# One attention step of TensorE in another order, in a fused AdaLN, attention and FFN kernel in three-pass float32

## The reference, cut to what matters

```python
x = x + attn(einsum('bct,bcd->bdt', x, W[style_id]))   # q,k,v projections, clip at 8, layer norm of q and k,
                                                       # 32 heads of 16, ALiBi, causal softmax, output projection
x = x + ffn(einsum('bsi,boi->bso', x, W2[adapter_id])) # up, relu squared, down, routed low-rank part, layer norm
```

## Time and profile before

| | |
|---|---|
| time, median of 3 runs | 1191.57 us (1190.74 to 1194.24) |
| the profiled execution | 1193.86 us, its span 1192.1 us |
| mean granted TensorE clock | 0.988 |
| attention loop in the span | from about 20 us to 627 us, steps 6 to 31 from 107 us on |
| busy: PE, PEld, DVE, ACT, POOL | 96%, 76%, 54%, 46%, 59% |

### The profile page before, as it was taken

One profiled execution on the slowest core, in us unless ns is written; L12 is line 12 of the kernel. 1 busy time (PEld: TensorE's weight loads), 2 busy tenths in 40 slices (PEclk: granted clock), 3 DMA queues, 4 the chain that ended last, 5 costly groups with the idle time before them and its releaser, 6 DMA issues.

```text
span 1192.1 us, 27390 instructions
## 1 busy us (share of the span) xinstructions
PE 1140.6 (96%) x11124; PEld 904.8 (76%) x11124; DVE 644.7 (54%) x1047; ACT 551.9 (46%) x910; POOL 705.1 (59%) x610
## 2 busy tenths in 40 slices
PE   6999999999999999999998999999999999999994
PEld 4777777777777777777776778787878878787883
DVE  5567565656575666565657444443444444443432
ACT  4365666666666666565665332315142332313120
POOL 4366778787878787878673545545545445433332
PEclk9999999999999999999998999999999999999998
DMA  7124545455554545344355732141412212120101
GB/s 272 45 66 164 187 160 171 166 185 171 166 178 158 180 160 188 123 150 122 134 190 215 264 135 97 62 133 71 137 62 91 91 53 89 54 89 14 58 18 44
DMA packets 60172, 152.38 MB, mean 128 GB/s; under 512 B 11280, under 2 KB 12048, under 8 KB 54672
## 3 DMA queue, kind: packets, MB, share of 16 engines
q1 hardware_dynamic: 42576, 106.06, 26.1%
q0 software_dynamic: 12224, 34.10, 8.7%
q10 hardware_dynamic: 5248, 10.49, 2.5%
HBM read 98.16 MB, written 38.27 MB: 114 GB/s over the span
## 4 chain that ended last, share of the span: by engine, by line
PE 92%; DMA 2%; issue 2%; DVE 2%; ACT 1%; POOL 0%; SPq 0%; ACTq 0%; DVEq 0%
PE bank L546 23%; PE pair L731 15%; PE bank L707 14%; PE bank L635 9%; PE bank L724 7%; PE bank L586 7%; PE pair L609 3%; PE bank L536 3%; PE pair L564 3%; PE bank L594 2%; PE bank L621 2%; DMA yt<-y_rows 1%; PE bank L576 1%; PE bank L670 1%; PE bank L680 1%
## 5 line engine op out<-in xcount | busy, mean ns | idle before, releaser
L1508 POOL TENSOR_TENSOR w_lo<-w2t,w_hi 128x2048 fp32r<-128x2048 f32 x38 | 175.8, 4625 | 11.5 <-ACT w_hi L888 11.5
L546 PE MATMUL bank<-wqkv_hi,h_hi 128*128 128x512 f32 x384 | 159.3, 415 | 3.3 <-ACT q_hi L986 2.0
L546 PE MATMUL bank<-wqkv_hi,h_lo 128*128 128x512 f32 x384 | 151.5, 395 | 0.2 <-issue 0.2
L546 PE MATMUL bank<-wqkv_lo,h_hi 128*128 128x512 f32 x384 | 150.6, 392 | 0.0
L1560 POOL TENSOR_TENSOR u_lo<-act,u_hi 128x512 fp32r<-128x512 f32 x64 | 82.4, 1288 | 109.7 <-ACT u_hi L1058 106.5
L1595 POOL TENSOR_SCALAR fve<-fmv 128x1 f32<-128x1 f32 x32 | 24.7, 772 | 153.3 <-DVE fmv L1420 153.3
L1502 POOL TENSOR_TENSOR probs<-probs,row_max 128x1024 f32<-128x1024 f32 x32 | 61.5, 1922 | 90.8 <-DVE row_max L1167 90.7
L1360 DVE TENSOR_TENSOR act<-act 128x512 f32<-128x512 f32 x64 | 54.9, 858 | 97.3 <-ACT act L1054 97.3
L707 PE MATMUL bank<-yT_hi,up_hi 128*128 128x512 f32 x256 | 102.7, 401 | 0.0
L731 PE MATMUL pair<-down_hi,u_hi 128*128 128x512 f32 x256 | 100.9, 394 | 0.0
L731 PE MATMUL pair<-down_hi,u_lo 128*128 128x512 f32 x256 | 100.8, 394 | 0.0
(11 more groups left out here) (172 smaller groups left out, 2920.0 us busy)
## 6 DMA issues: line engine op xcount, KB each, us to landing
w2t<-in_w SPq DMA_DIRECT2D x38, 1024.0 KB
vx<-v_hl SPq DMA_DIRECT2D x128, 68.0 KB
x_rows<-x1t SPq DMA_DIRECT2D x32, 256.0 KB, 4.6
yt<-y_rows SPq DMA_DIRECT2D x8, 1024.0 KB, 6.5
x1g<-x_rows SPq DMA_DIRECT2D x32, 256.0 KB, 3.2
kx<-k_hl SPq DMA_DIRECT2D x124, 64.0 KB
ffn_high<-w_high SPq DMA_DIRECT2D x20, 256.0 KB, 4.1
ffn_low<-w_low SPq DMA_DIRECT2D x20, 256.0 KB, 4.8
```

Source lines behind the costliest of these rows:

```text
L546: m = e.matmul(into, a[:, c, :], b[:, n, c, :], start=(c == 0 and k == 0), stop=(c == KC - 1 and k == 2))
L1508: e.tensor_tensor(w2_lo[:, :, :], w2t[:, :, :], w2_hi[:, :, :].bitcast(F32), ALU.subtract).then_inc(d_wlo, 1)
```

## The change

TensorE's step gets another order: q, values half, k, values half, turn of the slot, v, adapter, turn of the values, turn of q, turn of k, style(i+1), scores half, output, scores half. So v and the adapter are one run of 24 wide matmuls, the three turns and the style product follow each other, and the style product of a tile comes at the end of the step before its projections instead of a step earlier. The waits follow: the style product now waits for the `low_slot` of the same step, and a slot's turn for the `hlo` of one tile less. ACT puts `slot_out` before `high_o` and moves `high_h` from the step's start to behind `scale_k`; DVE moves `low_h` from behind the clip of q to behind `low_o`, and `low_o` behind `bn_aggr`. SP's and POOL's queues are unchanged, and so are all amounts of work.

```diff
@@ TensorE, style(t)
-                if t > LAG + 1:
-                    e.wait_ge(d_tl, t - LAG - 1)
+                if t > LAG:
+                    e.wait_ge(d_tl, t - LAG)
@@ TensorE, turn_slot(s)
-                    upto(e, "hlo", min(s + LAG + 1, T - 1))
+                    upto(e, "hlo", s + LAG)
@@ TensorE, the loop (the tests of live(i) are dropped too)
-                if 0 < i < T - 1:
-                    style(i + 1)
...
                 if i == 0:
                     make_route(2)
-                    style(1)
...
+                project(i, 2, B5, "pv")
+                if slot:
+                    adapt_slot(i - LAG, B2)
                 if live(i - 4):
                     turn_values(i - 4)
                 if live(i - 1):
                     upto(e, "ck", i)
                     turn_qk(i - 1, qn[(i - 1) % 2], "qn", B3, "tq")
-                if slot:
-                    adapt_slot(i - LAG, B2)
-                if live(i - 1):
                     upto(e, "cv", i)
                     turn_qk(i - 1, kn[(i - 1) % 2], "kn", B5, "tk")
+                if i + 1 < T:
+                    style(i + 1)
                 if live(i - 2):
                     scores(i - 2, 0)
@@ ScalarE, the loop
-                if live(i + 1):
-                    high_h(i + 1)
...
-                if live(i - 4):
-                    high_o(i - 4)
...
+                if i >= LAG:
+                    slot_out(i - LAG, B2)
+                if live(i - 4):
+                    high_o(i - 4)
                 if live(i - 1):
                     scale_q(i - 1, B3)
                     scale_k(i - 1, B5)
-                if i >= LAG:
-                    slot_out(i - LAG, B2)
+                if live(i + 1):
+                    high_h(i + 1)
                 if 0 <= i - 4 < CHUNKS:
                     high_chunk(i - 4)
@@ VectorE, the loop
-                if live(i + 1):
-                    low_h(i + 1)
...
-                if live(i - 4):
-                    low_o(i - 4)
...
                 m.then_inc(A["aggr"], 1)
+                if live(i - 4):
+                    low_o(i - 4)
+                if live(i + 1):
+                    low_h(i + 1)
```

More of the change, by code:

```diff
@@ L756, in _ @@
                 slot = i >= LAG
-                if 0 < i < T - 1:
-                    style(i + 1)
[L759 to L763, removed]
+                upto(e, "cq", i - 1)
+                if i > LAG:
+                    e.wait_ge(d_mc, i - LAG)
+                project(i, 0, B2, "pq")
                 if i == 0:
                     make_route(2)
-                    style(1)
                 if live(i - 4):
                     values(i - 4, 0)
[L769 to L773, removed]
+                upto(e, "ck", i - 1)
+                upto(e, "qhi", i - 2)
+                upto(e, "qlo", i - 2)
+                project(i, 1, B3, "pk")
                 if i == 0:
@@ L779, in _ @@
                     turn_slot(i - LAG, B7)
[L780 to L786, removed]
+                if i == 0:
+                    e.wait_ge(s_tables, 2)
+                upto(e, "cv", i - 1)
+                upto(e, "khi", i - 2)
+                upto(e, "klo", i - 2)
+                project(i, 2, B5, "pv")
+                if slot:
+                    adapt_slot(i - LAG, B2)
                 if live(i - 4):
```

## The result

Eleven runs each: 1192.37 us before (1190.24 to 1195.37), 1196.97 us after (1194.34 to 1199.59), a ratio of 1.0041 (95% interval 1.0027 to 1.0055). The change costs some 4.9 us (3.2 to 6.6). The forecast was +1.4 us: the range of the prediction held, but the loss is about three times what was forecast.

A forecast was written before the change was run, and what follows sets the result against it. POOL's chain, ending in the scatter that stalls the second scores, was taken to set the 19.80 us period. Profiled 1193.86 + 6.3 (first steps) - 4.9 (weights) = 1195.3; on the runs' scale 1191.57 + 1.4 = 1193.0 us, range 1185 to 1200.

The forecast's parts named there:

- The bound: Late steps: POOL's chain from scores to scatter sets the 19.80 us period; TensorE's own work is about 19.35.
- TensorE's order at 0: From step 6 on: the new order leaves the period at 19.80 us where weights are in time, 0 us.
- Rival B: Gather's pause falls into the narrow run and delays the first scores beyond the slack: 8.7 us, 1201.7; chance 0.15.
- rival E: Three turns and the style product let TensorE's clock fall in each step: +42 us, 1235; chance 0.02.
- the two more: First steps: between 0 and 2 further half-clock spells possible, 1.7 us each, beside the one expected.
- C: Scatter comes clear of the last scores, so TensorE's 19.35 us is the period: -11 us, 1182; chance 0.09.
- D: First steps overlap better (half of 6.3) and fewer switches help TensorE a little: 1187.6 us; chance 0.09.
- The late weights: Adapter's weights load 1.5 to 1.8 us earlier, ending POOL's 8 waits for them: gain 4.9 us, bound 2.5.
- The first steps: Turn of k, scale_k, high_h, low_h, q lie open without cover in the first steps: +6.3 us, range 4 to 9.
- the style product's 0.9: First steps: one style product now lies ahead of the first bound scores rather than behind: +0.9 us.
- Rival A: DVE's residual add slips behind ACT's high_h, delaying POOL's chain 0.3 us a step: 7.5 us, 1200.5; chance 0.15.
- the issuing stops TensorE's supply: Second scores: while POOL issues the indirect DMA, TensorE gets no new instructions; stall of 0.45 us a step.

The follow-up runs named there:

- all_three: Changed kernel, style product, high_h and low_h in old places in steps 0 to 5, scatter behind the scores, DVE's low_chunk in the next step: 1175.65 us.
- chunk_late: Changed kernel with DVE's low_chunk moved to the next step, behind the clip of q: 1195.78 us, ratio 1.0026 to the kernel before.
- scatter_late_new_b: Changed kernel with POOL's scatter waiting for the step's scores, run a second time: 1189.08 us, ratio 1.0126 to the kernel before.
- second pair: Traces of the kernel before and the changed kernel, both unchanged, run again on one chip: 1191.39 and 1196.74 us.
- scatter_late_old: Kernel before with POOL's scatter waiting for the step's scores: 1173.38 us, ratio 0.9994 to the kernel before.
- before_again: Kernel before, unchanged, run again for a trace: 1191.39 us, ratio 0.9994.
- style_early_old: Changed kernel with the style product, high_h and low_h in their old places in steps 0 to 5: 1180.80 us, ratio 1.0058.

## Why the prediction was right, and where it was off

**The bound.** Right: on the kind of chip that takes 1192 us the loop through POOL and the stop in the second scores set steps 6 to 31 in both orders. With the scatter behind the scores, in all_three, stop and loop are gone together and TensorE's own 19.30 is left; the prediction had worked out 19.35. Its sentence that only the second scores stop, 26 times, counts 4 stops of the first scores in; the bound does not depend on it.

**TensorE's order at 0.** Right: 19.79 to 19.91 in steps 8 to 28 after, 19.80 to 19.85 in the undisturbed steps before. Rival B (the gather's pause) did not come. Nor did rival E: the granted clock is 1.00 from step 6 to 600 us in all fourteen traces. In the first steps both traces of the change have the one spell of before (0.89 in step 2); the two more that the prediction held possible stand in chunk_late and scatter_late_new_b, so an execution of this order can have them. C did not come by itself either; it is what all_three brings about by hand. D had the wrong sign: the first steps overlap worse than worked out.

**The late weights, -4.9.** 4.8 in the first pair of traces, 2.0 in the second. The mechanism was right: no such wait is left after the change, and the load is issued 1.5 us earlier. Its size is that of one execution, and how much the median has is not known. This is the first term that was too kind.

**The first steps, +6.3.** The term that was mis-sized, though within its bounds of 4 to 9. By q of step 4 6.2 us were lost in both pairs, where the step-by-step sum of the prediction gives 5.8. The split was another: from the starts of k, the four steps cost 1.0, 2.6, 0.35 and 1.7 us, worked out as 1.2, 1.3, 1.55 and 1.75. The reason is the spell at the lower clock, with starts 0.43 us apart in place of 0.23. It covered seven matmuls of k in step 2 before (51.16 to 53.72) and six of q and the first of k after (50.91 to 53.47), so it moved a loss of about 1.2 us from one side of k's start to the other and left the sum. The 0.4 that were to come back did not in the first pair, and 0.6 more went in steps 5 and 6. In the second pair 1.1 came back in step 4 (17.94 us before, 16.86 after), and 0.7 went again. With the style product's 0.9 and the 0.6 of the last steps, where the scatter meets the first scores, the loss is 8.4 us in the first pair, in place of 6.3. That last part the prediction had not seen at all: it took the scatter's place in a step as fixed, while in the last steps the gathers ahead of it are gone.

**Sum.** First pair: +6.9 - 4.8 + 1.5 and 0.5 given back behind the loop make the 3.1 us of the span. Second pair: +5.8 - 2.0 + 1.4 + 1.0 behind the loop make 6.2. The medians, +4.6 and +4.0, lie between. What was given or lost behind the loop was not followed up.

**Rival A.** Not on the chips of the result, where POOL's loop leaves 0.5 us of slack to everything else; real on the others, 0.3 us a step in 18 steps, by the traces there; the edit that takes it away ran only on the chip of 1192 us.

## What to carry to other kernels

A steady step that keeps its period says nothing of the fill: what a later product hides in the loop lies open in the first steps, and here that was 6 us. The place of a pause decides its price: a scatter of 1.10 us stretched every burst of small matmuls that it met by some 0.5 us, and nothing once it was issued under wide ones. Removing one bound uncovers the next: with the stop gone DVE's chunk held the new order at 19.6 us, halfway between POOL's 19.84 and TensorE's 19.3, so the edits have to be tried together, and on the chip where the bound is. Before an effect is read off two traces, the granted clock of the same steps has to be compared: one spell more or less is 1.1 to 1.7 us.

## What was not expected of the hardware

Two kinds of chip, 1.6% apart on the same kernel (1192 and 1174 us). POOL's and DVE's larger operations take the same time on both, to 0.01 us in the mean (scatter_late_old against before_again). The difference seen in the traces is in the burst of small matmuls under POOL's indirect DMA: stretched in 26 of 26 steps on the one (mean length of the burst 1.12 and 1.10 us in two traces of before), never on the other (mean 0.58 in both traces of style_early_old, under the same overlap). The prediction's sentence that the issuing stops TensorE's supply therefore fits one kind only: the scatter's issue takes 1.10 to 1.11 us on both. On that kind all_three supports it, since the stop went when the scatter moved. Why it stops TensorE on one kind is open. A change is worth something else on the two: +0.4% measured on the one; on the other 1.2% for the kernel with one more wait.
